# Three MLP phases of a four-layer megakernel: each chunk multiplied once in plain float32 in place of three rounded terms

## The reference

```
L0:  x = x + gate * (gelu(modulate(layernorm(x)) @ W1 + b1) @ W2 + b2)
L1:  x = x + (gelu(film(rmsnorm(x))              @ W1 + b1) @ W2 + b2)
L2:  x = x + gate * modulate(layernorm(gelu(x @ W1 + b1) @ W2 + b2))
```

## Time and profile before

| | us |
|---|---|
| median of 3 runs (3930.34 to 3931.61) | 3930.72 |
| the profiled execution | 3926.93 |
| its span, first to last instruction | 3925.1 |
| TensorE busy | 3291.2 (84%) |
| VectorE busy | 2291.2 (58%) |
| ScalarE busy | 1729.5 (44%) |
| GpSimd busy | 513.8 (13%) |
| mean granted clock of TensorE | 0.922 |

### The profile page before, as it was taken

How to read it: one execution, slowest core, us unless ns; L and a number is a source line. 1 busy time by engine, 2 the same in 40 slices (tenths; PEclk the granted TensorE clock), 3 DMA queues, 4 the chain that set the end, 5 groups by cost and what they waited for, 6 DMA issues and landing times. The chain is left out here.

```text
span 3925.1 us, 74223 instructions
## 1 busy us (share of the span) xinstructions
PE 3291.2 (84%) x27690; PEld 2698.3 (69%) x27690; DVE 2291.2 (58%) x4337; ACT 1729.5 (44%) x3098; POOL 513.8 (13%) x519
## 2 busy tenths in 40 slices
PE   4999999997978869899997894999989899843686
PEld 2777777776977759777776783666666666632576
DVE  3555665555656656567775565565565655446464
ACT  1444344434533225445553553566565655400353
POOL 0000000000101001212232110110101101010243
PEclk8999999998988879999998996999999999855798
DMA  4000000001000000100000101000000000110243
GB/s 144 4 5 5 5 5 3 5 6 36 21 25 0 0 23 0 42 19 0 0 0 0 39 21 51 1 0 0 0 0 0 0 0 0 61 50 0 68 114 66
DMA packets 63631, 80.65 MB, mean 21 GB/s; under 512 B 9570, under 2 KB 56546, under 8 KB 63284
## 3 DMA queue, kind: packets, MB, share of 16 engines
q1 hardware_dynamic: 57412, 71.13, 6.1%
q0 software_dynamic: 6144, 8.52, 1.1%
HBM read 66.80 MB, written 12.85 MB: 20 GB/s over the span
## 5 line engine op out<-in xcount | busy, mean ns | idle before, releaser
L1431 ACT ACTIVATE L0a_prob<-L0a_st 128x512 f32<-128x512 f32 x256 | 138.7, 597 | 180.4 <-PE L0a_st L1638 180.4
L1431 ACT ACTIVATE L3a_prob<-L3a_st 128x512 f32<-128x512 f32 x256 | 138.8, 597 | 145.4 <-PE L3a_st L1638 145.4
L1881 DVE TENSOR_REDUCE L0a_mx<-L0a_s 128x2 f32<-128x512 f32 x256 | 164.7, 685 | 53.4 <-PE L0a_s L1614 48.1
L1881 DVE TENSOR_REDUCE L3a_mx<-L3a_s 128x2 f32<-128x512 f32 x256 | 164.5, 684 | 38.1 <-PE L3a_s L1614 36.6
L2174 ACT ACTIVATE L2a_prob<-L2a_st 128x512 f32<-128x512 f32 x256 | 132.3, 604 | 117.4 <-PE L2a_st L2214 117.4
L1359 POOL TENSOR_TENSOR L3a_shift<-L3a_neg,L3a_mx 128x256 fp32r<-128x256 f32 x128 | 87.3, 682 | 699.2 <-DVE L3a_mx L1881 699.2
L2451 DVE TENSOR_REDUCE L2a_mx<-L2a_s 128x2 fp32r<-128x512 f32 x256 | 163.5, 681 | 15.5 <-PE L2a_s L2214 15.5
L1860 DVE TENSOR_TENSOR L0a_qk_lo<-L0a_st,L0a_qk_hi 128x512 fp32r<-128x512 f32 x128 | 87.5, 691 | 88.1 <-ACT L0a_qk_hi L1395 88.1
L1871 DVE SCALAR_TENSOR_TENSOR L3a_qk_lo<-L3a_raw,cols_sb,L3a_qk_hi 128x256 fp32r<-128x256 f32 x256 | 124.6, 537 | 19.1 <-ACT L3a_qk_hi L1422 18.6
L3138 ACT ACTIVATE moe_xt<-moe_xm 128x1024 fp32r<-128x1024 f32 x8 | 8.5, 1056 | 277.8 <-DVE moe_xm L3235 277.8
L1669 PE MATMUL L3a_o<-L3a_prob,L3a_v 128*64 128x256 f32 x1024 | 124.6, 385 | 0.0
(11 more groups left out here) (607 smaller groups left out, 11988.1 us busy)
## 6 DMA issues: line engine op xcount, KB each, us to landing
moe_stage<-in_moe_w SPq DMA_DIRECT2D x16, 1024.0 KB, 5.9
x_sb<-in_x SPq DMA_DIRECT2D x1, 4096.0 KB, 24.2
L0a_gate<-gate_rows SPq DMA_DIRECT2D x32, 128.0 KB, 3.8
L0m_gate<-gate_rows SPq DMA_DIRECT2D x32, 128.0 KB, 3.8
L2a_gates<-gate_rows SPq DMA_DIRECT2D x2, 2048.0 KB, 12.4
L2m_gate<-gate_rows SPq DMA_DIRECT2D x32, 128.0 KB, 3.9
out_x<-x_sb SPq DMA_DIRECT2D x1, 4096.0 KB, 14.8
token_rows<-x_sb SPq DMA_DIRECT2D x1, 4096.0 KB, 26.4
```

The source lines that it names most:

```text
L1431: A(prob[:, u % 4, h, :], st_ps[u % 2][h][:], ACT.Exp, scale=64 ** -0.5).then_inc(p_done, 1)
L1881: V.tensor_reduce(mx[:, u % 2, h, :], s_ps[h][:].rearrange("p (t n) -> p t n", t=TT), AX.X, ALU.max).then_inc(mx_done, 1)
```

## The change

In mlp, the weights, tokens and GELU outputs are kept once, as float32, and each chunk is multiplied once, by a matmul on float32 operands. The copies and subtractions that made the parts are gone, and so are the staging buffers: the four pieces of the weights go straight to their places, all DMAs issued at the start, each with a semaphore of its own. TensorE's first up product waits for the two pieces of W1 and for xm, its first down product for the two of W2. On VectorE the body of a block has no loop over m any more: moments, normalise, add and modulate stand one after another. The attention phases, the routing and the experts stay as they are. The core of the diff:

```diff
-        w1 = [sb(f"w1{j}", [P, KD, MLP], F32R) for j in range(2)]
-        w2 = [sb(f"w2{j}", [P, MC, D], F32R) for j in range(2)]
-        stage = sb("stage", [P, 2, 1024])
+        w1, w2 = sb("w1", [P, KD, MLP]), sb("w2", [P, MC, D])
-        xt = [sb(f"xt{j}", [P, KD, NN], F32R) for j in range(2)]
-        h32 = sb("h32", [P, 2, NN])
-        h = [sb(f"h{j}", [P, MC, NN], F32R) for j in range(2)]
+        h = sb("h", [P, MC, NN])
...
         @block.sync
-            loader(sp=sp)[0]()
+            for (src, dst), done in zip(pieces, landed):
+                sp.dma_start(dst, src).then_inc(done, 16)
...
         @block.scalar
-            x_hi(0)
-            loader(act=act)[1]()
-            def body(i, more):
+            with act.Fori(0, IT) as i:
                 for m in range(MC):
                     act.wait_ge(up_done, MC * i + m + 1)
-                    if m >= 2:
-                        act.wait_ge(hlo_done, MC * i + m - 1)
-                    nc.scalar.activation(h32[:, m % 2, :], up_ps[m % 2][:], ACT.Gelu,
+                    nc.scalar.activation(h[:, m, :], up_ps[m % 2][:], ACT.Gelu,
                                          bias=...).then_inc(gelu_done, 1)
-                    act.wait_ge(gelu_done, MC * i + m + 1)
-                    nc.scalar.activation(h[0][:, m, :], h32[:, m % 2, :], ACT.Copy).then_inc(hhi_done, 1)
-                if more:
-                    x_hi(i + 1)
...
         @block.tensor
             transposes(0)
-            pe.wait_ge(lo_done, KD)
+            for done in landed[0:KD]:
+                pe.wait_ge(done, 16)
             def body(i, more):
-                pe.wait_ge(xlo_done, i + 1)
+                pe.wait_ge(xm_done, i + 1)
                 for m in range(MC):
                     if m >= 2:
                         pe.wait_ge(gelu_done, MC * i + m - 1)
                     for k in range(KD):
-                        last = three(up_ps[m % 2][:], [w[:, k, m * P:(m + 1) * P] for w in w1],
-                                     [x[:, k, :] for x in xt], k == 0, k == KD - 1)
+                        last = mm(up_ps[m % 2][:], w1[:, k, m * P:(m + 1) * P], xm[:, k, :], ...)
                     last.then_inc(up_done, 1)
                 pe.wait_ge(down_free, i + 1)
-                pe.wait_ge(lo_done, len(pieces))
+                for done in landed[KD:]:
+                    pe.wait_ge(done, 16)
                 for m in range(MC):
-                    pe.wait_ge(hlo_done, MC * i + m + 1)
+                    pe.wait_ge(gelu_done, MC * i + m + 1)
                     for tt in range(T4):
-                        last = three(down_ps[tt][:, 0:D], [x[:, m, tt * P:(tt + 1) * P] for x in h],
-                                     [w[:, m, :] for w in w2], m == 0, m == MC - 1)
+                        last = mm(down_ps[tt][:, 0:D], h[:, m, tt * P:(tt + 1) * P], w2[:, m, :], ...)
...
         @block.vector
-                dve.wait_ge(xhi_done, j + 1)
-                V.tensor_tensor(xt[1][:], xm[:], xt[0][:].bitcast(F32), ALU.subtract).then_inc(xlo_done, 1)
-            loader(dve=dve)[2]()
             def body(i, first, more):
-                for m in range(MC):
-                    dve.wait_ge(hhi_done, MC * i + m + 1)
-                    V.tensor_tensor(h[1][:, m, :], h32[:, m % 2, :], h[0][:, m, :].bitcast(F32), ALU.subtract)\
-                        .then_inc(hlo_done, 1)
-                    if m == 3 and more:
-                        normalise(i + 1)
-                    if late and not first and m == 1:
-                        res.moments(i - 1)
-                    if late and not first and m == 5:
-                        res.add(i - 1, the_gate)
+                if late and not first:
+                    res.moments(i - 1)
+                if more:
+                    normalise(i + 1)
+                if late and not first:
+                    res.add(i - 1, the_gate)
                 if more:
                     modulate(i + 1)
```

More of the change, by code:

```diff
@@ L2532, in mlp @@
             [pb(f"down{j}") for j in range(T4)]
-        w1 = [sb(f"w1{j}", [P, KD, MLP], F32R) for j in range(2)]
-        w2 = [sb(f"w2{j}", [P, MC, D], F32R) for j in range(2)]
-        stage = sb("stage", [P, 2, 1024])
+        w1, w2 = sb("w1", [P, KD, MLP]), sb("w2", [P, MC, D])
         xn, xm = sb("xn", [P, T4, D]), sb("xm", [P, KD, NN])
-        xt = [sb(f"xt{j}", [P, KD, NN], F32R) for j in range(2)]
         stats, mv = sb("stats", [P, T4, 6]), sb("mv", [P, T4, 2])
         ve, ve2, rstd, rstd2 = sb("ve", [P, T4]), sb("ve2", [P, T4]), sb("rstd", [P, T4]), sb("rstd2", [P, T4])
-        h32 = sb("h32", [P, 2, NN])
-        h = [sb(f"h{j}", [P, MC, NN], F32R) for j in range(2)]
+        h = sb("h", [P, MC, NN])
         y, y2 = sb("y", [P, T4, D]), sb("y2", [P, T4, D])
         gate, y_bias = sb("gate", [P, BB, 2, D]), sb("y_bias", [P, D])
-        landed = [sem("landed0"), sem("landed1")]
-        hi_done, lo_done = sem("hi_done"), sem("lo_done")
+        landed = [sem(f"landed{n}") for n in range(KD + 2)]
         stats_done, aggr_done, ve_done, rstd_done, xn_done = (sem(x) for x in ("stats", "aggr", "ve", "rstd", "xn"))
-        tp_done, xm_done, xhi_done, xlo_done = sem("tp"), sem("xm"), sem("xhi"), sem("xlo")
-        up_done, gelu_done, hhi_done, hlo_done = sem("up"), sem("gelu"), sem("hhi"), sem("hlo")
+        tp_done, xm_done, up_done, gelu_done = sem("tp"), sem("xm"), sem("up"), sem("gelu")
         down_done, down_free, ep_done, ep_step, xh_done = (sem(x) for x in ("down", "down_free", "ep", "ep_step", "xh"))
@@ L2555, in mlp @@
         for k in range(KD):
-            pieces.append((t[nm + "_w1"][k * P:(k + 1) * P, :], w1[0][:, k, :], w1[1][:, k, :], False))
+            pieces.append((t[nm + "_w1"][k * P:(k + 1) * P, :], w1[:, k, :]))
         for m in range(0, MC, 4):
[L2558 to L2561, removed]
+            pieces.append((t[nm + "_w2"][m * P:(m + 4) * P, :].rearrange("(c p) n -> p c n", p=P), w2[:, m:m + 4, :]))
         extra = 16 if nm == "L2m" else 0
@@ L2630, in _ @@
             b1 = COL_AT[{"L0m": "L0_cond_b1", "L1m": "L1_cond_mlp_b1", "L2m": "L2_cond_fc1_b"}[nm]]
-            def x_hi(j):
-                act.wait_ge(xm_done, j + 1)
-                nc.scalar.activation(xt[0][:], xm[:], ACT.Copy).then_inc(xhi_done, 1)
-            x_hi(0)
-            loader(act=act)[1]()
-            def body(i, more):
+            with act.Fori(0, IT) as i:
                 for m in range(MC):
                     act.wait_ge(up_done, MC * i + m + 1)
-                    if m >= 2:
-                        act.wait_ge(hlo_done, MC * i + m - 1)
-                    nc.scalar.activation(h32[:, m % 2, :], up_ps[m % 2][:], ACT.Gelu,
+                    nc.scalar.activation(h[:, m, :], up_ps[m % 2][:], ACT.Gelu,
                                          bias=g["cols"][:, b1 + m:b1 + m + 1]).then_inc(gelu_done, 1)
-                    act.wait_ge(gelu_done, MC * i + m + 1)
-                    nc.scalar.activation(h[0][:, m, :], h32[:, m % 2, :], ACT.Copy).then_inc(hhi_done, 1)
-                if more:
-                    x_hi(i + 1)
-            with act.Fori(0, IT - 1) as i:
-                body(i, True)
-            body(IT - 1, False)
         @block.tensor
@@ L2657, in _ @@
             mm = nc.tensor.matmul
[L2659 to L2663, removed]
             def transposes(j):
@@ L2681, in body @@
                     for k in range(KD):
-                        last = three(up_ps[m % 2][:], [w[:, k, m * P:(m + 1) * P] for w in w1],
-                                     [x[:, k, :] for x in xt], k == 0, k == KD - 1)
+                        last = mm(up_ps[m % 2][:], w1[:, k, m * P:(m + 1) * P], xm[:, k, :], start=(k == 0), stop=(k == KD - 1))
                     last.then_inc(up_done, 1)
                 pe.wait_ge(down_free, i + 1)
-                pe.wait_ge(lo_done, len(pieces))
+                for done in landed[KD:]:
+                    pe.wait_ge(done, 16)
                 for m in range(MC):
-                    pe.wait_ge(hlo_done, MC * i + m + 1)
+                    pe.wait_ge(gelu_done, MC * i + m + 1)
                     for tt in range(T4):
-                        last = three(down_ps[tt][:, 0:D], [x[:, m, tt * P:(tt + 1) * P] for x in h],
-                                     [w[:, m, :] for w in w2], m == 0, m == MC - 1)
+                        last = mm(down_ps[tt][:, 0:D], h[:, m, tt * P:(tt + 1) * P], w2[:, m, :], start=(m == 0), stop=(m == MC - 1))
                     if m == 3 and more:
```

## The result

| | before | changed |
|---|---|---|
| median, us | 3930.53 (3928.65 to 3931.61, 4 runs) | 4019.41 (4017.48 to 4027.48, 4 runs) |
| ratio, 95% interval | | 1.0231 (1.0213 to 1.0248) |
| profiled execution / its span | 3926.93 / 3925.1 | 4018.35 / 4016.5 |

The changed kernel is 2.3% slower, 88.9 us by the medians and 91.4 us by the profiled executions. The forecast was +92.8 us between the profiled executions, and a median of 4023 us.

What follows compares the result with a forecast made beforehand. The prediction took TensorE's stream to bound the MLP blocks: 123.1 us more for plain products, less 30.3 given back at starts and in L2m, is +92.8 us, a median of 4023 us; own range 4010 to 4034, wider range 4006 to 4060.

Steps and rivals of the forecast that it cites:

- The unit price of a plain product: MLP up and down: plain records spaced 0.43 us at 512 columns and 0.2155 at 256, two for each product.
- rival (a): MLP blocks: plain records cost some ns more, a block of 29.40 us, +116.6 us, total 4047 us; chance 15%.
- Four units for three: TensorE in MLP blocks: four units of work replace three, a block 28.41 us against 23.28, +123.1 us over three phases.
- rival (c): MLP blocks: a plain product is two records as cheap as rounded ones, block 15.80 us, -210 us, total 3721; chance 3%.
- Rival (b): MLP blocks: a plain product costs four rounded matmuls, block 30.75 us, +149 us, total 4080 us; chance 6%.
- Weight loads: Up and down on TensorE: 96 stationary loads a block against 144, about 190 ns each, stay hidden.
- What went from VectorE and ScalarE: Removed copies and subtractions return nothing in steady blocks, except L2m's 0.52 us in each of 7 blocks, 3.6 us.
- The starts: MLP phase starts: first product 4.8 us earlier, first GELU stall gone; with L2m's blocks 30.3 us given back.
- the ends of phases don't change: Ends of the MLP phases: last products, residual and barrier take as long as before.
- The term of the low clock: First up part of each MLP phase: 1.2 GHz through 5.1 us of products, costing 2.5 us, between 1.5 and 3.5.
- rival (d): MLP blocks: the clock falls to 1.2 GHz under plain products, +680 us, total about 4700 us; chance 3%.
- The sum: Whole kernel: 123.1 - 30.3 = +92.8 us, profiled execution 4019.7 us, median 4023 us, 2.4% slower; chance 71%.

Runs made afterwards that it cites:

- e3: Changed kernel's order of work with three rounded matmuls, all on the same rounded operands, for each plain one, no splits; 3895.95 us, 0.9913 of the kernel before.
- e9: Like e3 but with two rounded matmuls for each chunk, low terms of the result left out; 3728.51 us in a single run.
- e8: Changed kernel with each up product cut into two of 256 moving columns; 4019.93 us in a single run.
- e6: Kernel before, all three terms and splits kept, with four staging and four GELU output buffers, W1 first, reordered ScalarE and VectorE starts; 3907.60 us, ratio 0.9945.
- e5: Changed kernel with the DMAs of W2 issued only when both pieces of W1 have landed; 4023.71 us in a single run.

## Why the prediction was right

**The unit price of a plain product** carried the sum, and held: 0.43 and 0.2155 us from the conditioning and L1a, 0.429 and 0.216 measured in place. The block was forecast at 28.41 us and is 28.42. The 16-column stationary operand of the earlier trace rows did not matter, and rival (a) falls. One reading there was shakier than the prediction says: the conditioning's plain records start 0.85 us apart up to about 50 us and 0.43 after, while the clock column gives 1.00 for both, so the column can't be relied on there. That 0.43 belongs to 2.4 GHz rests on the factor of two and on L1a. The matmuls' whole price, with the splits gone on both sides, is the 24 x 5.13 = 123.1 us between e3 and the changed kernel, as forecast.

**Four units for three.** e9 shows what rival (c) would have been: two rounded records for each product make a block of 16.3 us, and the plain kernel's blocks take 28.42. Rival (b), four rounded matmuls, is too dear by 2.3 us a block: a rounded record takes 13 ns more than its columns at 2.4 GHz, at 512 and at 256 columns, and a plain one 2 to 3 ns. The break-even of 0.36 in rival (c) is 0.35 for the blocks alone and 0.37 with the starts, which changes nothing. The Trainium skill's four passes (FP8 and Floating Point Precision, TensorE Precision Notes) agree as a count; as a price the rows of plain records decided.

**Weight loads** stayed hidden with 96 loads of a full 128x128 operand in a block, and with 128 in e8. The rule of the Trainium skill (TensorE: Matmul & The Clock Gate, Part 3, What overlaps and what doesn't) that loads overlap matmuls in flight only when the row group differs is not what these runs show.

**What went from VectorE and ScalarE** gave nothing inside the blocks of L0m, shown by e3's 23.29 us. L2m's 0.52 us a block came back, in the changed kernel and in e6, which kept the splits and among its edits has four buffers for the GELU output in place of two.

**The starts** gave back 30.3 us by the forecast and 24 x 5.14 - 93.0 = 30.4 measured, and that they agree so closely is luck: two errors cancel. The first is in L2m. In L0m and L1m the first product stood 3.96 us behind the transposes, as worked out, and 4.8 us earlier after the phase's start. In L2m it came 3.8 us earlier and not 4.8. I had W1 landed by 2164.1, which is 4.2 us from its issue, and the first product could not start before 5.45. The own range had allowed for this, but for another reason (W2 in the same queue), and e5 shows that reason to be 0.3 us of it at most. The step that I left out is the one from the last byte to the start of the product that waits, 0.8 us in e5. The second error is in "the ends of phases don't change": from TensorE's last product to the next phase it is 5.05, 3.84 and 11.11 us after in place of 5.34, 4.13 and 11.39, which is 0.9 us together; the reason is open. The split of the 92.8 us into phases was also a little off by its own terms, which give 33.5, 30.8 and 28.5 us. The term of the low clock was 2.5 us for each phase; the first up parts of 16.52, 16.00 and 16.06 us less 13.73 make it 2.8, 2.3 and 2.3. These stretches of L0m after show it, columns as in the earlier trace rows, the clock third from the end, against the earlier trace rows:

```profile
936.00:938.00 2.00, 2.00 (x4) 0.85 (x3) 0.74 (x7) 0.00 (x0) 1.19 (x2) 0.50 0.00 0
938.00:940.00 2.00, 2.00 (x3) 0.66 (x2) 2.00 (x1) 0.69 (x1) 2.00 (x1) 0.50 0.00 0
940.00:942.00 2.00, 2.00 (x6) 0.92 (x5) 1.25 (x4) 0.69 (x1) 0.13 (x1) 0.93 0.00 0
```

About 5.5 us of products run at 1.2 GHz there, and the level rises with plain products alone; rival (d) falls, and the steady block above stands at 1.00. In L1m before, TensorE's wait of 3.4 us on the GELU was followed by a second stretch at 0.50, from 1464.67 to about 1470 us, and that went with the wait.

**The sum** was 92.8 us, and the three phases measured 93.0. Between the profiled executions the difference is 91.4; the other 1.6 us lie in phases that the change doesn't touch. The median came out 3.6 us under the 4023, since the step from the profiled execution to the median, 3.8 us before, was 1.1 us for the changed kernel.

## What to carry to other kernels

Before a product is put into another form, look for one record of that form anywhere in the trace and take its distance from start to start, not its length or its number: here the two records of a plain float32 product cost 0.86 us at 512 columns, four rounded ones 0.91 and the three that they replaced 0.68. Work that goes from engines beside a full TensorE returns only at the starts, where TensorE waits for it, and here a better order gave two thirds of that, 19 of 30 us, without touching the arithmetic (e6). If accuracy allows fewer rounded terms, the first one left out is worth 7.0 us a block in L0m (23.28 to 16.32), and the second 5.45 (to 10.87), since the GELU is the bound by then.

## What the runs showed of the hardware

- A rounded matmul of 512 columns is spaced 0.227 us and a plain record of the same columns 0.429, less than twice as much: the rounded one has 13 ns over its columns at 2.4 GHz, with or without the splits beside it (e3), and the plain one 2 ns. Why is open.
- 1 MB in two DMAs takes 5.1 us from issue to the first product that waits for it, alone in the queue, and for the last 0.8 us of these it moves nothing (e5). In e6's L0m the first 512 KB were in use 3.7 us after the issue.
- Cutting a plain matmul of 512 columns into two of 256 is almost free: 64 records take 13.81 us (e8), 32 take 13.73.
